# Windowed attention on TensorE: 32-query tiles over a block-diagonal k instead of a masked q

## What is computed

```python
q = Wq @ layernorm(x) + bq;  k = Wk @ cond + bk;  v = Wv @ cond + bv      # per block, [128, 1024]
k, v = pad(k, 8 left, 7 right), pad(v, 8 left, 7 right)
dots = einsum('bhdt,bhdtw->bhtw', q, k[windows of 16]) * 16 ** -0.5
out  = einsum('bhtw,bhdtw->bhdt', softmax(dots), v[windows of 16])
x = x + tanh(g_xattn) * (Wo @ out + bo)
h = layernorm(x)
x = x + tanh(g_ffn) * ((silu(h @ gate) * (h @ up)) @ down)                # 1024 -> 3584 -> 1024
```

## Time and profile before

| | us |
|---|---|
| median of 3 runs | 1858.68 |
| lowest, highest | 1848.99, 1859.18 |
| the profiled execution, its time | 1863.79 |
| the profiled execution, its span | 1862.0 |
| mean granted clock of TensorE | 0.962 |

### The profile page before, as it was taken

The page is one execution under the profiler, slowest core; times in us unless marked ns, Lnnn a source line. Parts: engine busy times, 40 slices in busy tenths (PEclk is TensorE's granted clock), DMA queues, the critical chain, the costliest instruction groups (busy, mean ns, idle before and its releaser), DMA issues.

```text
span 1862.0 us, 39744 instructions
## 1 busy us (share of the span) xinstructions
PE 1706.6 (92%) x14534; PEld 937.4 (50%) x14534; DVE 1541.5 (83%) x1466; ACT 997.7 (54%) x1278; POOL 1546.8 (83%) x848
## 2 busy tenths in 40 slices
PE   3898988889885799999999999999999999999996
PEld 2777777777774344444444444444444443444444
DVE  2466666666662799999999999999989999999996
ACT  1455555655553355655556555556555555565552
POOL 3467767767665699999999999999999998999975
PEclk7799999999996899999999999999999999999998
DMA  4353443534432322222222222222222222222127
GB/s 105 86 132 92 119 111 103 128 100 103 126 92 60 102 77 74 75 74 75 79 70 80 70 80 70 79 70 80 69 73 76 80 69 70 77 71 74 51 91 271
DMA packets 160555, 166.84 MB, mean 90 GB/s; under 512 B 11630, under 2 KB 127022, under 8 KB 160330
## 3 DMA queue, kind: packets, MB, share of 16 engines
q1 hardware_dynamic: 160346, 164.07, 31.0%
HBM read 113.92 MB, written 16.78 MB: 70 GB/s over the span
## 4 chain that ended last, share of the span: by engine, by line
PE 75%; DVE 11%; issue 6%; POOL 5%; SPq 1%; ACT 1%; DMA 1%; DVEq 0%; POOLq 0%; ACTq 0%
PE bank L1103 51%; DVE acc L888 6%; PE bank L1004 6%; PE bank L973 3%; PE bank L1032 3%; PE bank L1015 3%; PE bank L962 3%; POOL oacc L557 2%; PE bank L967 2%; DVE pT L806 1%; PE bank L1043 1%; PE bank L977 1%; DVE xT L845 1%; PE bank L993 1%; DVE rmax L794 1%
## 5 line engine op out<-in xcount | busy, mean ns | idle before, releaser
L888 DVE SCALAR_TENSOR_TENSOR acc<-bank,scale,acc 128x1024 f32<-128x1024 f32 x784 | 952.7, 1274 | 49.8 <-PE bank L1103 31.9
L1103 PE MATMUL bank<-xT,w_int 128*128 128x512 f16 x3584 | 858.6, 382 | 28.4 <-issue 11.7
L557 POOL TENSOR_TENSOR oacc<-oacc,d_part 128x1024 f32<-128x1024 f32 x336 | 796.3, 2370 | 64.1 <-ACT d_part L731 50.5
L731 ACT ACTIVATE d_part<-bank,scale 128x1024 f32<-128x1024 f32 x336 | 374.0, 1113 | 416.3 <-PE bank L1103 398.8
L1103 PEld LDWEIGHTS bank<-xT,w_int 128*128 128x128 f16 x3584 | 346.4, 98 | 470.0 <-issue 36.3
L1103 PE MATMUL bank<-h_hi,d_int 128*128 128x512 f16 x896 | 340.7, 380 | 10.9 <-DVE acc L888 5.1
L1103 PE MATMUL bank<-h_lo,d_int 128*128 128x512 f16 x896 | 340.1, 380 | 0.0
L499 POOL TENSOR_TENSOR raw_z<-raw_w,raw_z 128x512 int32<-128x512 int32 x168 | 247.5, 1474 | 20.5 <-DMA raw_z<-in_L_ffn_up_z_dram 16.8
L485 POOL CAST p_hl<-pr 128x768 f16<-128x768 f32 x64 | 52.8, 825 | 158.7 <-ACT pr L618 158.7
L1103 PEld LDWEIGHTS bank<-h_hi,d_int 128*128 128x128 f16 x896 | 87.6, 98 | 143.4 <-DVE acc L888 38.3
L794 DVE TENSOR_REDUCE rmax<-bank 128x16 f32<-128x768 f32 x64 | 61.3, 957 | 102.6 <-PE bank L1004 102.6
(11 more groups left out here) (86 smaller groups left out, 1636.8 us busy)
## 6 DMA issues: line engine op xcount, KB each, us to landing
raw_w<-in_L_ffn_gate_w_dram SPq DMA_DIRECT2D x56, 256.0 KB, 3.0
raw_z<-in_L_ffn_gate_z_dram SPq DMA_DIRECT2D x56, 256.0 KB, 3.6
raw_w<-in_L_ffn_up_w_dram SPq DMA_DIRECT2D x56, 256.0 KB, 3.0
raw_z<-in_L_ffn_up_z_dram SPq DMA_DIRECT2D x56, 256.0 KB, 3.6
raw_w<-in_L_ffn_down_w_dram SPq DMA_DIRECT2D x56, 256.0 KB, 2.6
raw_z<-in_L_ffn_down_z_dram SPq DMA_DIRECT2D x56, 256.0 KB, 3.5
vt<-vn_hl SPq DMA_DIRECT2D x64, 220.0 KB
row<-in_x_dram SPq DMA_DIRECT2D x16, 512.0 KB, 3.9
```

Source lines behind the costliest of these rows:

```text
L557: nc.gpsimd.tensor_tensor(into, into, part, ALU.add).then_inc(d_added, 1)
L731: nc.scalar.activation(d_part[:, (count(0, x, False) - 1) % 2, :], pair[slot][:, :, :].rearrange("p h r -> p (h r)"), ACT.Copy, scale=scal ...
L888: nc.vector.scalar_tensor_tensor(out=into, in0=pair[u % 4][:, :, :].rearrange("p h r -> p (h r)"), scalar=scale[:, par, i, m, k:k + 1], in ...
L1103: last = nc.tensor.matmul(dst[:, h, :], weights, rows_of(h, part), start=(part == 0), stop=(part == 1))
```

## The change

Layout. q is no longer masked or moved: `q_hl` keeps plain q, double-buffered. k is moved instead (`move_k`, again eight transfers) into `km`, where each head's 16 rows hold k in its own column range and zeros elsewhere. A scores matmul now takes 32 contiguous weight columns (the queries of one tile) over 64 rows and moves 4 x 48 = 192 columns; eight such matmuls (four query tiles, two halves of the rows) lie in eight different parts of the array. There are again 64 a step; the mask takes eight matmuls instead of two.

Values. They get a column of ones (`V1 = 17`), so the row sums come with the mix. A mix matmul takes 32 weight columns and moves 17 columns: 128 a step, in place of 32 + 16. `pick`, `row_sums`, `scale_o` and `turn_o` are gone. DVE's `normalize(n-2)`, ahead of `soften(n)`, inverts 16 sums a row and multiplies 256 elements a row; PE turns the result by four fp32 transposes (task `t`, two a block), and DVE copies it.

Order. `mix(n-1)` stays at the end of step n, and only the last one moves behind the first units of the feed-forward part. ACT now does `exp(n)` first, then the high parts of `before`, then both halves of `take_pT(n-1)`. ACT also takes over the two normalizations from POOL. The ring of projection banks grows from two to three. The weights of the projections are loaded first and from ACT's queue, `wo` by one transfer instead of eight and its column by one instead of eight. All 14 passes are written out; there is no loop.

```diff
@@ tasks
-            return ((v[:2], v[2:]), (q[:1], q[1:]), (x[:1] + k[:1], k[1:]), (x[1:], o))[s]
+            return ((x_end + k[:1], k[1:]), (q[:1], q[1:] + t[:1]), (v[:2], v[2:] + t[1:]), (x, o))[s]
@@ banks
-        proj, score, mixed = bank[0:2], bank[2:4], bank[6:8]
+        proj, score, mixed = (bank[0], bank[1], bank[7]), bank[2:4], bank[6]
@@ scores
-                for j in range(JQ):
-                    for of_q in range(2):
-                        for of_k in range(2):
-                            for hg in range(2):
-                                last = nc.tensor.matmul(dst[hg][:, j, :], q_of[of_q][r, at::NJ],
-                                                        k_hl[b % 2][r, of_k, t:t + KW], start=False, ...)
+                tiles = [(jj, hg) for jj in range(JJ) for hg in range(2)]
+                for jg in range(JG):
+                    for of_q in range(2):
+                        for of_k in range(2):
+                            for jj, hg in tiles:
+                                r, c = slice(GC * hg, GC * hg + GC), slice(QB * jj, QB * jj + QB)
+                                dst = score[hg][c, jg * HG * KW:(jg + 1) * HG * KW].rearrange("p (h k) -> p h k", k=KW)
+                                last = nc.tensor.matmul(dst, q_hl[b % 2][r, of_q, t:t + QB], km[b % 2][r, of_k, :, t:t + KW], ...)
@@ mix
-                            last = nc.tensor.matmul(mixed[hg][:, j * GC:(j + 1) * GC],
-                                                    pT[0:2 * KW, n % 2, hg, j * P:(j + 1) * P],
-                                                    vt[b % 2][0:2 * KW, slot_of(at), part, hg * GC:(hg + 1) * GC], ...)
+                for jg in range(JG):
+                    for h in range(HEADS):
+                        for part in range(2):
+                            for jj in range(JJ):
+                                last = nc.tensor.matmul(
+                                    mixed[c, to:to + V1], pT[0:2 * KW, n % 2, h // HG, at:at + QB],
+                                    vt[b % 2][0:2 * KW, slot_of(JQ * s + JJ * jg + jj), part, h, :], ...)
@@ ACT, one step
-                    if n >= 2:
-                        pick(n - 2)
+                    if s == 0 and b + 1 < B:
+                        norm_x(b + 1)
+                    exp(n)
                     before, after = tasks_of(b, s)
                     for t in before:
                         take_high(*t)
                     if n:
                         take_pT(n - 1)
-                    exp(n)
                     for t in after:
                         take_high(*t)
+                    if s == 1 and b >= 2:
+                        norm_row(b - 2)
@@ take_pT on ACT (DVE's copy is removed)
-                nc.scalar.activation(pT[0:2 * KW, n % 2, 0, :], turned[0][0:2 * KW, :], ACT.Copy).then_inc(pT_ready[0], 1)
+                for hg in range(2):
+                    last = nc.scalar.activation(pT[0:2 * KW, n % 2, hg, :], turned[hg][0:2 * KW, :], ACT.Copy)
+                last.then_inc(pT_ready, 1)
@@ DVE, one step
+                    if n >= 2:
+                        normalize(n - 2)
                     soften(b, s)
-                    if n:
-                        take_pT(n - 1)
@@ start
+            for dst, src, loaded in ((wk, WkT, wk_loaded), (wq, WqT, wq_loaded), (wv, WvT, wv_loaded), (wo, WoT, wo_loaded)):
+                act.dma_start(dst[:, :], src).then_inc(loaded, 16)
@@ passes
-            one(0, 0, True, False)
-            with eng.Fori(0, (NC - 2) // 2) as i:
-                one(2 * i + 1, 1, False, False)
-                one(2 * i + 2, 0, False, False)
-            one(NC - 1, 1, False, True)
+            for c in range(NC):
+                one(c, c % 2, c == 0, c == NC - 1)
```

More of the change, by code:

```diff
@@ L418, in one @@
                         load_piece(c + 1, n)
-            passes(sp, one)
+            passes(one)
             for b in range(B):
@@ L583, in one @@
                         add_down(c, x)
-            passes(pool, one)
+            passes(one)
             low_hidden(NC, -1)
@@ L761, in one @@
                         take_scales(c + 1, 1 - par)
-            passes(act, one)
+            passes(one)
             high_hidden(NC, -1)
@@ L941, in one @@
                         hidden(c, u // QU)
-            passes(dve, one)
+            passes(one)
             for n, (kind, x) in enumerate(end):
@@ L1036, in mix @@
-                last.then_inc(mix_ready, 1)
-            def row_sums(n):
-                for hg in range(2):
-                    for j in range(JQ):
-                        at = JQ * KW + n % S * JQ + j
-                        last = nc.tensor.matmul(score[hg][:, at:at + 1], pT[0:2 * KW, n % 2, hg, j * P:(j + 1) * P],
-                                                ones16[0:2 * KW, :], start=True, stop=True, skip_group_check=True)
-                return last
-            pe.wait_ge(zeroed, 6)
@@ new lines, in mix @@
+                last.then_inc(mix_ready, 1)
+            pe.wait_ge(zeroed, 4)
+            pe.wait_ge(masks_made, 8)
+            pe.wait_ge(wk_loaded, 16)
+            for t in first_tasks[:2]:
+                project(*t)
+            pe.wait_ge(wq_loaded, 16)
+            for t in first_tasks[2:4]:
+                project(*t)
+            pe.wait_ge(wv_loaded, 16)
+            for t in first_tasks[4:]:
+                project(*t)
+            pe.wait_ge(wo_loaded, 32)
+            nc.tensor.matmul(mixed[:, 0:1], wo[:, :], bv_col[:, :], start=True, stop=True).then_inc(bias_turned, 1)
@@ L1144, in one @@
                             pe.wait_ge(*emptied(c, u))
-                        for n in range(2):
-                            project(*last_at[u], n)
+                        for t in last_at[u]:
+                            project(*t)
+                    if first and u == LAST_MIX:
+                        mix(S * B - 1)
                     if u % 3 == 2 and x is None:
@@ L1153, in one @@
                     if first and u == 1:
-                        pe.wait_ge(rinv_ready, B)
-                    if first and u == 3:
-                        pe.wait_ge(picked, S * B)
-                    if first and u == LAST_X + 1:
-                        for half in range(2):
-                            pe.wait_ge(pT_ready[half], S * B)
+                        pe.wait_ge(shifted, S * B)
+                    if first and u == LAST_MIX + 1:
+                        pe.wait_ge(normalized, S * B)
                     wait = emptied(c, u)
@@ L1166, in one @@
                         down(c, x, par if x >= 0 else 1 - par, u % 4)
-            passes(pe, one)
+            passes(one)
             for n, (kind, x) in enumerate(end):
```

481 lines of the change are left out of this document (226 added, 255 removed).

## The result

The changed kernel takes 1903.08 us (median of 4 runs, 1901.41 to 1903.48) against 1857.77 of the kernel before: a ratio of 1.0255, with a 95% interval of 1.0227 to 1.0284. It is slower by 45 us. The forecast was 1969, so 110 us slower; the sign was right and the size was not.

What follows compares the result with a forecast made beforehand. The prediction took PE to bound a step before the change and a ring through DVE and ACT after it. Span: 1862.0 + 154 - 24 - 8 - 12 = 1972 us, 1974 of time, 1969 by the median; range 1835 to 2045.

Steps and rivals of the forecast that it cites:

- The ring: Each attention step: scores, maximum, subtraction, exp, high parts, copies, mix without overlap; 22.4 us a block on DVE and ACT.
- The cover: PE's projections and transposes, about 3.5 to 4.5 us a step, fit under the ring's 5.3 to 5.9 us, costing nothing.
- The price of a pair: Each weight load with its matmul in scores and mix takes 25 ns: scores 2.1 us, mix 3.2 us a step.
- the forecast's lower bound: 12.5 ns a pair in scores and mix, if two pairs run in one spacing: +14 us.
- Rival 1: Array parts take scores and mix pairs side by side, 12.5 ns or less: 1832 us, 1829 by the median; chance 0.22.
- +154: Growth of the 61 steady attention steps in us: a block of four takes 43.6 us in place of 33.5.
- The clock: A lower PE clock in attention: +82 us if all runs at 1.2 GHz; put into the range, not the sum.
- The stretch that the forecast calls all narrow: A stretch before the change with PE busy 3.50 of 3.50 us, followed by one at clock 0.51.
- The start: Earlier wo transfers and k projected first: third scores about 24 us earlier than 63.27, at least 10, at most 30.
- The end: After attention POOL loses 3.80 us of normalizing and the scaling behind it: -8 us, 0 to -10.
- The loop: Passes written out remove PE's five waits without releaser at the branches: -12 us, or 0 if straight-code fetching costs as much.

Runs made afterwards that it cites:

- x1: The changed kernel with the mix's 128 pairs reordered, all of one query tile (one column part), then the next: 1946.9 us, one run.
- x2: The changed kernel without the low part of the values in the mix, 64 pairs a step in place of 128: 1803.2 us, one run.
- x6: The changed kernel with pT's copies shared by ACT and DVE, ACT's ahead of exp, and projections `after` between the mix's halves: 1854.0 us, ratio 0.9974.
- x10: The kernel before with its passes written out and its own mix cut into four column parts: 1996.5 us, one run.
- x4: The kernel before with its 14 passes written out, nothing else: 1834.7 us, ratio 0.9888.
- x11: x8_both with the second of the projections `after` moved behind the second half of the mix: 1837.4 us, ratio 0.9885.
- x9_before_flat_wo: The kernel before with its passes written out and the sixteen transfers of wo and its column ahead of q's move: 1829.0 us, ratio 0.9832.
- x8_both: x6 with the transposes of p also directly behind the scores, ahead of the projections `before`: 1829.9 us, ratio 0.9849.

## Why the prediction came out as it did

**The ring: right in its links, its length and its price, wrong in that it closes in every step.** PE waits for pT in 56 of the 61 steps, 87.4 us or 1.6 a step that waits, where about 2 were forecast. In 28 steps the way from the end of the scores through maximum, subtraction, exp, high parts and copies to the mix has no gap, and takes 5.46 us (4.8 to 5.8), for a forecast mean of 22.4 / 4 = 5.6. In 19 steps ACT's copies wait for PE's transposes instead; in 12 DVE's maximum starts 0.2 to 1.1 us late behind `normalize`, which the forecast gave as possible when the scores are as short as 0.8 us (they take 0.84); in 2 ACT's normalization stands ahead of exp. The chain goes through the maximum in 23 steps, not in 61. One reading beside it was off: 1.07 us is one matmul of line 973 and not a half of q, which takes two of them, 1.97 us before and 1.12 after. The cover was long enough even so in two steps of three.

**The price of a pair: wrong, and this is the step that carried the error.** "I take 25 ns for every pair, narrow or not." It was read from pairs that follow each other on the whole array. x1 measures the same 25 ns on one column part and 9 on four in turn, which is also under the 12.5 ns of the forecast's lower bound. Scores and mix take 2.3 us a step, not 5.3: 3.0 x 61 = 183 us too much in the sum. Rival 1 had this mechanism, with a chance of 0.22; I weighed the scores' 30 ns against it, though they had two row halves to alternate and weight loads of their own, at a stride (164 ns each on average, 94 for the narrow ones of the mix; what of it is the stride was not tried), and gave too little to the two masks that ran side by side. The Trainium skill, TensorEngine Tiling (Array Packing), Key Properties, says that different tiles of the array load weights and multiply independently of each other; x1 and the changed kernel agree, as far as the 25 ns that become 9.

**A term that the forecast put at nothing: the instructions come late.** 90 us, in 47 waits. Rival 1, right on the price, would have had 1829 us and missed by more than the forecast did. The queue that brings instructions, first before, then after:

```profile
q8 instruction: 130, 2.13, 0.5%
```

```profile
q8 instruction: 159, 2.61, 0.6%
```

159 packets for 20166 pairs, so for 40332 instructions and those for semaphores, are about 256 instructions each; the MB of the row over the packets is 16 KB. Three things tie the waits at a packet's end to these packets. First, in each of the eleven kernels that has any, every such wait (499 in all, the single one of the kernel before among them) has the same remainder when PE's instructions ahead of it, with weight loads and those for semaphores, are counted and divided by 256. Second, each of the 499 ends 1.1 to 1.9 us behind the end of the last packet of this queue (1.4 in the median). Third, in the changed kernel the packet that PE waits for starts 1.3 us (median) after PE has begun the packet ahead of it, takes 1.0 us, and PE goes on 1.4 us behind it: from PE's first instruction of a packet to its first of the next are 3.7 us in the median of the 47, half of them between 3.4 and 4.1. The 3.3 us of my expectations are at the low end of that. In the kernel before no 256 of PE's instructions in the steps pass in under 4.35 us; in the changed one the fastest take 1.0 and the mix, which is 256 instructions, 1.2. So the waits shrink, go and come with the number of instructions in a short time: 16 us where the mix is slow (x1), 20 where it has half as many (x2), 68 where it is cut (x6), 76 in a kernel that had none (x10). The Trainium skill, Runtime: NRT & Kernel Launch, Instruction fetch mechanics, says that instructions come in blocks of 16 KiB, the next while the current one runs, and that this is mostly hidden because they are issued more slowly than they arrive. The block size and the order agree with the trace; that it is hidden holds before the change and not after it.

**The clock: in the range, not in the sum.** The mean in the steps fell from 0.95 to 0.82. The edit of x10 does as much to the kernel before (0.95 to 0.81), with some 85 us of busy time in matmuls that it leaves alone. Whether the narrow matmuls do that or PE's stops between them isn't separated, and how much of the changed kernel's 88 us is the clock isn't either: no run holds the clock while the rest changes. The stretch that the forecast calls all narrow also ends with 0.9 us of a half of q (line 973 from 222.12 us).

**The other terms.** The start: -19.3 for -24, inside the 10 to 30 that were given. The end: -2.9 for -8. What holds it is not POOL's normalization. In both kernels POOL's last parts of p stand behind a subtraction of zero points (line 499, now 480) that waits for its transfer, 13.17 us before and 16.62 after, and PE's last transposes wait for POOL, 9.23 us before and 8.70 after. The loop: -24 in the passes for -12 (x4); the term was half of what it should be, because it was read from the gaps on PE, and DVE's behind them are longer.

In sum +154 was 183 too high for the pairs and 90 too low for late instructions, which leaves 61, against 88.4 measured. The other 27 us are not pinned down; the lower clock and the steps in which PE's own transposes come last are candidates, and the parts overlap, so this is an account and not a proof. Two errors of opposite sign kept the direction right, and that is luck: with the measured price of a pair the ring alone gives 22.4 + 4 x (1.12 + 1.18) = 31.6 us a block, 482 us for 61 steps, faster than the 510 before.

## What to carry to other kernels

Write down the ring of a pipelined step, from an engine's result back to its own next instruction, before counting busy time: here two copies on another place on ACT cost about 50 us, while PE's own work was less than before. A stretch of matmuls so cheap that 256 instructions pass in a microsecond is no longer bound by the array, since here the next packet of 256 can be begun only some 3.7 us after the one before. Look for waits without a releaser in the middle of a group and count the instructions between them. Making the matmuls fewer helped at once (x2); spreading them between long instructions shortened these waits (x6, x11) and helped the time only where nothing else stood behind them. Ask of each wait without a releaser what ended at that moment: some were waits for another engine. For this kernel the two cheapest gains were outside of the change: the passes written out and the start (x9_before_flat_wo, 1829 us) do as much as the changed kernel's order mended (x8_both, 1830 us).

## What the hardware showed that I had not expected

- A weight load with its matmul: 25 ns on one column part, 9 ns with four column parts in turn (128 pairs in 3.15 and in 1.18 us), with 17 moving columns; with 64, still 1.22 us.
- PE's instructions come in packets of 256. When one passes faster than the next comes, PE stops at its end until some 3.7 us from its beginning (47 waits, 90 us in the changed kernel); PE resumes 1.4 us behind the packet. With at least 4.35 us for any 256 (the steps of the kernel before) there is one such wait, of 1.1 us.
- Cutting the mix into narrow parts lowered the mean granted clock in the steps of the kernel before from 0.95 to 0.81 with the same result and the same other matmuls; the stops that came with it are part of the edit's effect. Another order of the changed kernel's instructions, with as narrow a mix, has 0.93 (x8).
- A loop of six turns cost 24 us in the passes, where PE's own waits at its branches sum to 12.
